# First unit of a convolution split by columns between two stages of a transformer block, with plane differences taken from PSUM

## The reference

```python
x = x + 0.5 * ffn(layernorm(x), ...)
x = x + attn(layernorm(x), conv_w, conv_b, wq, bq, ...)
x = x + 0.5 * ffn(layernorm(x), ...)

def ffn(x, weight, bias, gate_w, in_channel_scale, out_channel_scale):
    routing = softmax(x @ gate_w.T)                 # 8 experts
    in_scale = routing @ in_channel_scale
    out_scale = routing @ out_channel_scale
    return (x * in_scale) @ sign(weight).T * out_scale + bias

def attn(inputs, conv_w, conv_b, ...):
    x = conv1d(inputs, conv_w, padding='SAME') + conv_b   # 3 taps, 1024 -> 768 channels
    q, k, v = split(x, 3)
    # then attention with 16 heads in blocks of 128 tokens, and two projections
```

## Time and profile before

| | |
|---|---|
| time, median of 3 runs | 1028.48 us (1027.41 to 1028.79) |
| the profiled execution's own time | 1030.44 us |
| its span, first to last instruction | 1028.3 us |
| mean granted TensorE clock | 0.967 of full speed |
| busy: PE, DVE, ACT, POOL | 922.7, 707.2, 427.4, 372.2 us |

### The profile page before, as it was taken

How to read it: one execution, slowest core, us unless ns; L and a number is a source line. 1 busy time by engine, 2 the same in 40 slices (tenths; PEclk the granted TensorE clock), 3 DMA queues, 4 the chain that set the end, 5 groups by cost and what they waited for, 6 DMA issues and landing times.

```text
span 1028.3 us, 15188 instructions
## 1 busy us (share of the span) xinstructions
PE 922.7 (90%) x4960; PEld 700.5 (68%) x4960; DVE 707.2 (69%) x1469; ACT 427.4 (42%) x1127; POOL 372.2 (36%) x317
## 2 busy tenths in 40 slices
PE   3789999895999999999988998998899788999997
PEld 2466677673333677788767786777777666787786
DVE  5677776568898898655685488189459857667552
ACT  3534444331134326243664355255535544343331
POOL 2145555573543321000223142133133441554555
PEclk8899999997999999999989999999999899999999
DMA  9433322322333341684003022212152484333332
GB/s 283 157 123 123 124 83 82 144 82 73 109 107 124 132 148 68 225 293 177 2 11 92 9 75 83 62 41 71 51 142 75 165 251 138 123 123 145 122 121 106
DMA packets 43011, 119.97 MB, mean 117 GB/s; under 512 B 7232, under 2 KB 16448, under 8 KB 41536
## 3 DMA queue, kind: packets, MB, share of 16 engines
q1 hardware_dynamic: 42944, 119.11, 35.2%
HBM read 87.64 MB, written 31.46 MB: 116 GB/s over the span
## 4 chain that ended last, share of the span: by engine, by line
PE 51%; DVE 15%; issue 5%; ACT 3%; DMA 1%; POOL 0%; POOLq 0%; DVEq 0%; ACTq 0%; SPq 0%
PE a_p_g L1791 17%; PE a_p_g L619 11%; PE c_p_m L1237 4%; PE c_p_m L1239 3%; PE c_p_m L1241 3%; PE c_p_m L1240 3%; PE a_p_s L1815 2%; DVE a_sums L1691 2%; DVE a_s L1688 2%; PE a_p_o L1839 2%; ACT a_s L1587 1%; PE a_p_s L562 1%; PE a_p_t L1825 1%; DVE a_pt L1705 1%; DMA c_raw<-in_conv_w_dram 1%
## 5 line engine op out<-in xcount | busy, mean ns | idle before, releaser
L1520 POOL TENSOR_TENSOR a_s<-a_s,a_sums 128x512 f32<-128x512 f32 x64 | 66.7, 1042 | 281.0 <-DVE a_sums L1697 281.0
L272 POOL TENSOR_TENSOR f_y<-f_y,f_res 128x512 f32<-128x512 f32 x64 | 82.9, 1296 | 143.9 <-DVE f_y L474 143.4
L1587 ACT ACTIVATE a_s<-a_s,a_nmx 128x128 f32<-128x128 f32 x256 | 99.4, 390 | 42.4 <-DVE a_nmx L1693 42.4
L619 PE MATMUL f_p_m<-f_wsign,f_a_hi 128*128 128x512 f32 x256 | 106.2, 415 | 0.0
L1791 PE MATMUL a_p_g<-c_xs_hi,x_room 128*128 128x512 f32 x256 | 96.8, 426 | 9.7 <-DVE c_xs_lo L1653 9.0
L619 PE MATMUL a_p_g<-f_wsign,f_a_hi 128*128 128x512 f32 x256 | 103.4, 404 | 0.0
L619 PE MATMUL f_p_m<-f_wsign,f_a_lo 128*128 128x512 f32 x256 | 102.5, 400 | 0.0
L619 PE MATMUL a_p_g<-f_wsign,f_a_lo 128*128 128x512 f32 x256 | 101.1, 395 | 0.0
L1237 PE MATMUL c_p_m<-c_vf,c_ring_f 128*128 128x512 f32 x192 | 86.3, 606 | 9.5 <-DVE c_ring_f L902 6.8
L269 POOL TENSOR_TENSOR f_res<-f_res,f_hbias 128x512 f32<-128x512 f32 x64 | 84.2, 1315 | 8.4 <-DMA f_res<-x_after_attention 7.2
L1239 PE MATMUL c_p_m<-c_vh,c_ring 128*128 128x512 f32 x192 | 75.4, 393 | 5.1 <-issue 2.9
(11 more groups left out here) (219 smaller groups left out, 2177.4 us busy)
## 6 DMA issues: line engine op xcount, KB each, us to landing
c_raw<-in_conv_w_dram SPq DMA_DIRECT2D x24, 768.0 KB, 4.3
f_w_raw<-in_w_t_dram SPq DMA_DIRECT2D x8, 1024.0 KB, 11.8
f_res<-in_x_dram SPq DMA_DIRECT2D x16, 512.0 KB, 4.5
x_after_ffn<-f_y SPq DMA_DIRECT2D x8, 1024.0 KB, 6.3
f_xin<-x_after_attention SPq DMA_DIRECT2D x8, 1024.0 KB, 5.1
f_res<-x_after_attention SPq DMA_DIRECT2D x16, 512.0 KB, 4.5
out_dram<-f_y SPq DMA_DIRECT2D x8, 1024.0 KB, 6.3
f_xin<-in_x_dram SPq DMA_DIRECT2D x7, 1024.0 KB, 5.1
```

What stands on the lines that cost most here:

```text
L272: pool.tensor_tensor(y[:, p, t, h], y[:, p, t, h], res[:, t, h], ALU.add).then_inc(y_done, 1)
L619: last = pe.matmul(p_m[:, q % 2, :], part[p][:, k, q // 2 * P:q // 2 * P + P], wsign[:, k, q % 2 * HALF:q % 2 * HALF + HALF], start=(k == ...
L1520: pool.tensor_tensor(s[:, r], s[:, r], sums[:, r].unsqueeze(2).broadcast_to([P, 4, P]), ALU.mult).then_inc(probs_ready, 1)
L1587: done = act.activation(s[:, r, h, :], s[:, r, h, :], ACT.Exp, bias=nmx[:, r, h:h + 1], scale=SCALE, accum_out=sums[:, r, h:h + 1])
```

## The change

1. Both feed-forward and convolution programs go into one block: there is no barrier between them. The PSUM banks of the convolution's products (`c_p_m`) are shared with the feed-forward's `p_s`, `p_r` and `p_o`, the SBUF places are reordered.
2. `difference` replaces `differences`: after ACT has copied planes 0 and 1 of a piece (half as many elements as before), DVE subtracts them from planes 2 and 3 as they stand in the transposes' PSUM bank and writes the differences into X. It does this for all groups, 32 times in all; POOL does it no more. PE's next transposes into the same bank wait for DVE's difference, where they waited for ACT's copy. The last two groups use two banks.
3. Of unit 0, the first 384 of 512 columns (`EARLY`, the tokens of groups 0 to 5) are computed in the feed-forward's last part: DVE makes their data in four pairs of blocks (`early_data`, 8 instructions over two blocks each), PE runs 16 products of 384 columns (`early_product`) between the transposes of the last group. The remaining 128 columns follow (`late_data`, 4 instructions over four blocks each, and 16 products of 128 columns).
4. `ring_f` has six places instead of three (both halves of the later ring), and four filters instead of three are made within the feed-forward. The loads of `raw` for n = 2 and 3 are issued by SP around the last store, in place of after the barrier.

```diff
         def normed(g, p, c):
 
             pe.wait_ge(y_normed, g + 2 + (late(g) and c // 2))
-            wait(pe, n_copied, 4 * g + c + 1 - (late(g) and c > 0))
-            if late(g):
+            two = isinstance(g, int) and (g == NG - 1 or g == NG - 2 and c > 0)
+            wait(pe, n_differenced, 4 * g + c - two)
+            if two:
                 pe.wait_ge(t_copied, 4 * NG)
...
-            act.copy(Xp[:, k0:k0 + 4, :, quads], bank[:].rearrange("p (k s m) -> p k s m", k=4, s=4)).then_inc(n_copied, 1)
+            act.copy(plane_part(g, c, slice(0, 2)), normed_planes(g, c)[:, :, 0:2, :]).then_inc(n_copied, 1)
...
+        def difference(g, c):
+
+            dve.wait_ge(n_copied, 4 * g + c + 2)
+            dve.tensor_tensor(plane_part(g, c, slice(2, 4)), normed_planes(g, c)[:, :, 2:4, :], plane_part(g, c, slice(0, 2)),
+                              ALU.subtract).then_inc(n_differenced, 1)
...
+                if q == 3 and X is not None and exists(g - 1):
+                    difference(g - 1, 0)
+                    if late(g):
+                        conv.first_filter(dve, 0, 0)
+                    difference(g - 1, 1)
+                    if late(g):
+                        conv.first_filter(dve, 0, 1)
...
+                if q == 3:
+                    for t in range(FT):
+                        if exists(g + 4):
+                            tile_stats(g + 4, p, t)
+                        if X is not None and exists(g - 1):
+                            difference(g - 1, 2 + t)
+                        if X is not None and late(g):
+                            (last_stats, last_normalise)[t](0)
+                    if exists(g + 4):
+                        mean_var(g + 4)
+                if q == 1 and X is not None and late(g):
+                    dve.wait_ge(n_differenced, 4 * (NG - 2))
+                    conv.early_data(dve, Xp, 0)
...
+            group_loop(dve, f.body)
+            conv.early_data(dve, Xp, 1)
+            f.last_stats(1)
+            for c in range(2):
+                f.difference(NG - 1, c)
+            f.last_normalise(1)
+            for i in range(2):
+                conv.first_filter(dve, 1, i)
+            conv.early_data(dve, Xp, 2)
+            for c in range(2, 4):
+                f.difference(NG - 1, c)
+            conv.early_data(dve, Xp, 3)
+            dve.wait_ge(first.ends.differenced, 4 * NG)
+            for half in range(2):
+                conv.late_data(dve, Xp, half)
...
+            group_loop(pe, f.body)
+            for k in range(KD):
+                for n in range(2):
+                    conv.early_product(pe, p_s[:, n, 0:EARLY], k, n)
+                if k in (1, 3):
+                    f.normed(NG - 1, (NG - 1) % 2, k - 1)
+                    f.normed(NG - 1, (NG - 1) % 2, k)
...
+    def first_data(self, dve, Xp, ks, cols):
+
+        quads = slice(cols.start + 1, cols.stop + 1)
+        for f in range(2):
+            dve.scalar_tensor_tensor(self.vf[:, f, ks, cols], Xp[:, ks, 2, quads], -2.0 if f else 2.0, Xp[:, ks, 3, quads],
+                                     ALU.mult, ALU.add).then_inc(self.data_ready, ks.stop - ks.start)
...
         dve.wait_ge(self.outer_made, n + 1)
-        if i >= RING:
-            dve.wait_ge(self.chunk_used, self.used(i - RING))
...
+        if i >= 2 * RING:
+            dve.wait_ge(self.chunk_used, self.used(i - 2 * RING))
```

More of the change, by code:

```diff
@@ L281, in body @@
                     pool.tensor_tensor(nrstd[:, t:t + 1], nvpe[:, t:t + 1], minus_half[:, t:t + 1], ALU.pow).then_inc(n_rstd, 1)
+                if q == 2 and X is not None and late(g):
+                    conv.outer_sum(pool, 1)
         return PoolSteps(zero_gate, zero_scales, set_half, zero_routing, power, halve_bias, body)
@@ new lines, in _ @@
+        @block.sync
+        def _(sp):
+            f = first.sync(sp)
+            f.load_tiles()
+            f.load_x(1, 1)
+            f.load_gate()
+            f.load_scales()
+            f.load_w(0)
+            f.load_w(1)
+            f.load_bias()
+            f.load_x(2, 0)
+            f.load_w(2)
+            f.load_w(3)
+            for t in range(FT):
+                f.load_res(0, t)
+            f.load_x(3, 1)
+            group_loop(sp, f.body)
+            conv.load(sp, 2)
+            f.store(NG - 1, (NG - 1) % 2)
+            conv.load(sp, 3)
+            f.stored()
@@ new lines, in _ @@
+        @block.gpsimd
+        def _(pool):
+            f = first.pool(pool)
+            f.zero_gate()
+            f.zero_scales()
+            f.set_half()
+            f.zero_routing()
+            f.power(0)
+            f.power(1)
+            f.halve_bias()
+            f.power(2)
+            group_loop(pool, f.body)
+        @block.vector
+        def _(dve):
+            f = first.vector(dve)
+            f.start()
+            f.constants()
+            for g in (0, 1):
+                f.stats(g, g)
+                f.normalise(g, g)
+            f.round_scales()
+            f.part_scales()
+            f.softmax(0)
+            f.stats(2, 0)
+            for k in range(KD):
+                f.scale(0, 0, k)
+                if k:
+                    f.low(0, 0, k - 1)
+            f.low(0, 0, KD - 1)
+            f.normalise(2, 0)
+            f.softmax(1)
+            f.stats(3, 1)
+            group_loop(dve, f.body)
[13 more added lines that the diff above has]
+                conv.late_data(dve, Xp, half)
@@ new lines, in _ @@
+        @block.scalar
+        def _(act):
+            f = first.scalar(act)
+            for q in range(4):
+                f.copy_t(0, 0, q)
+            f.sign_w(0)
+            f.sign_w(1)
+            f.copy_logits(0)
+            for q in range(4):
+                f.copy_t(1, 1, q)
+            f.sign_w(2)
+            f.exponent(0)
+            f.sign_w(3)
+            f.copy_routing(0, 0)
+            for k in range(KD):
+                f.high(0, 0, k)
+            f.copy_logits(1)
+            for k in range(4, KD):
+                f.sign_w(k)
+            f.exponent(1)
+            for q in range(4):
+                f.copy_t(2, 0, q)
+            group_loop(act, f.body)
+            for c in range(4):
+                f.copy_normed(NG - 1, c)
@@ L805 @@
+    return first
 QUADS4 = T // 4
@@ L942, in _ @@
                 sp.dma_start(to[:], of).then_inc(conv.attention_biases, 16)
-            for n in range(2, PAIRS):
+            for n in range(4, PAIRS):
                 conv.load(sp, n)
@@ L968, in shift @@
                 pool.tensor_tensor(room[:, 1], plane(k, 0, 2), plane(k, 0), ALU.subtract).then_inc(shifted, 1)
+            pool.wait_ge(first.ends.differenced, 4 * NG)
             for k in range(KD):
@@ L1361, in attention_phase @@
         mask = sb("mask", [P, P], small + 128)
-        order = conv.room[:, 2, 0:P]
+        order = conv.room[:, 2, QUADS4 - P:QUADS4]
         p_s, p_t, p_g = ps("p_s", [P, 2, HALF]), ps("p_t", [P, 2, HALF]), ps("p_g", [P, 2, HALF])
```

241 lines of the change are left out of this document (78 added, 163 removed).

## The result

The changed kernel took 1019.9 us, median of 20 runs (1015.9 to 1022.4), the kernel before 1025.2 us on the same chip (20 runs, 1019.5 to 1030.9). The ratio is 0.9944, 95% interval 0.9930 to 0.9957: about 5.7 us faster. The forecast was 5.6.

The account below looks back on a forecast made before the run. DVE's time before filter 18 was taken to bound the convolution's first stage. A gain of 8.75 us there less 3.15 in the loop gives 5.6, from 1028.48 to 1022.9 us; range 1018.0 to 1027.5.

Parts of the forecast that it names:

- What bounds: Convolution's first stage: DVE's time before filter 18 sets its end, 20.9 us after filter 18 is ready.
- Idle time that can go: DVE from 217 us to filter 18: 12.25 us of idle time can go, of which 1.0 remains.
- without a gap over 1 us from about 225 us on: Sign after the change: DVE busy without such a gap, and no wait for a ring place.
- Work and collisions: DVE before filter 18: exchanged work adds 0.5 us, meetings with POOL 2.0 (0 to 5); filter 18 comes 8.75 earlier.
- Which part gives it: DVE's idle time: six ring places remove the wait at 263.54; early data, moved differences and no barrier remove the rest.
- PE keeps up: Convolution's unit 1 on PE starts near 256 us, five us before its limit of 261.4.
- The loop: Feed-forward groups 1 to 6: DVE's added differences cost 3.15 us in all, bounds 0 to 7.8.
- The 0.85 us a round for groups 1 to 3: Quarter 3 of these groups: delay behind L474 passes through to PE, 0.85 us a group.
- The 0.2 for groups 4 to 6: No statistics there; the hand-over from ACT's copy to DVE takes longer, 0.2 us a group.
- Rival (c): Early and small products on PE run at 1.2 GHz, unit 1 starts near 267; gain 0.1 us, 1028.4 us; chance 0.09.
- Clock 0.9 or more over the last group's end: Sign after the change: PE's granted clock stays at 0.9 or more there.
- all four rivals: More won, 1017.7 us (0.17); most given back, 1026.0 (0.17); clock throttled, 1028.4 (0.09); slower through the loop, 1032.3 (0.07).

Follow-up runs that it names:

- the repeated profile: The changed kernel run and profiled once more with no edit; 1020.5 us, ratio 0.9948 to the kernel before.
- the run with the third difference first: Changed kernel with DVE's third difference in quarter 3 ahead of all four statistics instructions, the fourth behind them; 1019.6 us, ratio 0.9949 to before.
- the run with the ring of three: Changed kernel without the column split and with three ring places, the fourth filter behind the data again; 1028.4 us, ratio 1.0028 to before.
- the shift on DVE: Changed kernel with POOL's sum for n = 2 earlier and block 0's two shifted sums on DVE; 1015.5 us, ratio 0.9902 to before.
- all mends: Changed kernel with differences of groups 0 to 5 on POOL, POOL's n = 2 sum earlier, block 0's shifted sums on DVE; 1014.8 us, ratio 0.9906 to before.

## Why the prediction was right, point by point

**What bounds.** Right: the stage ends 20.87 us behind filter 18 in every run above, and between 263 us and filter 18 DVE is busy for 50.96 of 51.86 us, PE for 44.87. That the wait at 263.54 was for a ring place was right too, though the row named POOL.

**Idle time that can go.** The term was mis-sized. I kept 1.0 us of 12.25; 4.09 stayed. The wait for a ring place went, but DVE still waits for POOL's sums (0.85 and 1.16 us at filters, 1.5 at the statistics of the output), for ACT (0.6 and 0.9) and for POOL's power (0.3). The sign "without a gap over 1 us from about 225 us on" failed by the 1.16.

**Work and collisions.** +0.5 and +2.0 forecast, +1.13 measured (89.65 to 90.78). The 12 data instructions took 12.3 us with their meetings (11.1 was forecast without). Other instructions took less than before, the 19 filters 21.4 us instead of 22.9, so that less was added than counted. Net 7.03 instead of 8.75, within the bounds given; the repeated profile has 7.7.

**Which part gives it.** Here the working pointed the right way and weighed wrongly. It counted 4.90 us for the ring place and gave the rest to the data in DVE's gaps and the barrier. The ring is 6.8 us, the split 0.65 to 1.3 and the barrier about 1, these two hardly above the scatter of S: without ring and split all else together loses 0.5 (104.25 against 103.79 of before).

**PE keeps up.** Right. Unit 1 starts near 258.5 (254.98 and 3.5 us of small products), which is the estimated 256 and the loop's 3; the limit moves with the loop too, to 264.4.

**The loop.** 3.15 forecast, 3.13 in the profile, 4.1 in the repeat. That 3.13 meets 3.15 is luck. The 0.85 us a round for groups 1 to 3 was right (0.89, 0.95 and 0.90 in the repeat). The 0.2 for groups 4 to 6 was too little: 0.34 for group 4's quarter with the three behind it, 0.53 and 0.52 for the last quarters of groups 5 and 6. And in the profile one round got back 1.0 us by a load that landed late. By last quarters alone the growth is 1.34 to 1.42 us in groups 1 to 3, but 0.44 of it is the shifted mark and comes off the next quarter. The wait of PE was 1.19 where 1.3 was forecast, and the forecast was right not to charge it, as the run with the third difference first shows.

**The clock.** Rival (c) fell as a rival, but happened in small: the window after the second pair's data,

```profile
242.20:244.16 1.96, 0.88 (x2) 0.32 (x3) 1.96 (x2) 0.00 (x0) 1.00 (x1) 1.00 0.03 10
244.16:248.03 3.87, 3.87 (x8) 2.01 (x9) 3.78 (x10) 0.00 (x0) 0.56 (x1) 0.56 0.66 266
```

has a granted clock of 0.56 of 2.4 GHz, close to the lower level of 1.2 GHz, and six records of early products take 3.87 us where eight took 2.75. "Clock 0.9 or more over the last group's end" was wrong there. It shows no cost: unit 1 still started 6 us ahead of its limit. The Trainium skill (TensorE: Matmul & The Clock Gate, section on oscillation) warned of short bursts between waits; this trace has one such place.

**From filter 18 to the end.** From the last scaling of group 0 to filter 18 the two profiles of the changed kernel are 3.97 and 3.54 us shorter than before's; the measured ratio says 5.7 (4.4 to 7.2). Taken from the 1028.48 us of the forecast it gives 1021.3 to 1024.1: the times of all four rivals (1017.7, 1026.0, 1028.4, 1032.3) lie outside. But that 5.6 met 5.7 so closely is partly luck: loop and stage gave 1.6 to 2.1 less than forecast, and some 2 us come from elsewhere. The run with the ring of three shows the same offset (4.35 us later at filter 18, 2.9 slower by its ratio), so it is neither ring nor split. What it is stays open: with one profile of before it can't be told from chance. In the 14 profiles the stretch ahead of L takes 57.8 to 61.1 us and the one behind filter 18 702.4 to 709.4, and before has 61.0 and 709.4.

## What to carry to other kernels

Where one engine's idle time ends in a wait for a buffer place, the place is the cheap cure: the places were worth 6.8 us here, the split of the work 0.65 to 2.3. Work moved into an engine's gaps is worth the gap less what it then loses beside its neighbour: here 3.3 to 3.7 us filled, 2.4 to 2.6 lost. And a wait that appears at an instruction is not yet its cost: change the order, and see if the sum of the round moves. Take the sum over a whole round, since a mark on one engine shifts with that engine's waits.

## What the runs showed of the hardware

- A POOL sum of two SBUF inputs that began within a stream of DVE instructions of two SBUF inputs each (512 and 768 columns) was held until the stream had ended, DVE unslowed: 5.19, 5.12 and 6.39 us instead of 1.3 where it began 0.1 to 0.2 us behind the head of the stream, 4.67 us with the shift on DVE and 4.21 with all mends. With a semaphore wait between DVE's instructions it took 1.91, and DVE's stream doubled. Beside data instructions of 1024 columns, without waits, neither was held for more than one: a DVE instruction took 1.21 us alone and up to 2.29 beside POOL, the eight 13.24 us beside four POOL instructions and 10.25 beside one, and POOL's took 2.0 to 2.3, here in the run without the split:

```profile
246.69 2.25 POOL L1017 TENSOR_TENSOR c_room<-X 128x512 f32<-128x512 f32 x1
```

  The Trainium skill (SBUF — State Buffer, section on who interferes with whom) has such a pair of instructions exclude each other for one whole instruction; the runs agree on the pairing, but here the loser waited through several. Why the 1024-column stream shares and the shorter one does not was not tried.
- A normalisation of one SBUF tensor (`TENSOR_SCALAR`, 128x1024) takes 0.81 us alone and two in a row 1.53; two took 2.50 to 2.54 wherever POOL's bias sum (128x512) began 0.12 to 0.69 us into them, and 1.53 where it began 0.81 us or more into them (16 and 11 cases).
- Of the 14 profiles, 6 have a dip of the clock in group 6 and 8 have none. The program ahead of it doesn't decide it: of the 9 profiles with the changed kernel's loop 4 have it, of the 4 with the differences on POOL 2. After a stretch in which PE was busy for 4.9 of 7 us, the granted clock was 0.68 in before and 1.00 in the run with the differences on POOL. The dip costs 1.5 us, more than most single edits here gave. Windows of before:

```profile
191.00:198.00 7.00, 4.89 (x23) 3.77 (x22) 5.17 (x13) 1.80 (x4) 5.39 (x5) 1.00 0.52 163
198.00:201.00 3.00, 3.00 (x12) 2.39 (x11) 1.13 (x4) 0.37 (x1) 2.88 (x3) 0.68 1.02 417
```

The same place in the run with the differences on POOL:

```profile
188.00:195.00 7.00, 4.89 (x23) 3.73 (x23) 5.11 (x13) 1.80 (x4) 5.33 (x5) 1.00 0.51 159
195.00:199.50 4.50, 4.50 (x22) 3.69 (x21) 2.16 (x6) 1.04 (x3) 2.96 (x3) 1.00 1.03 417
```
